# Spans of several edge groups, a wait for the products ahead of the one-hot rows, and a later place for one unit of the graph network

## The reference

```python
# layer 0
edge_input = concatenate([x[dst], x[src], edge_attr, u[batch[dst]]], axis=1)
messages   = relu(edge_input @ W1.T + b1)                      # 200000 x 128
aggregated = segment_sum(messages, dst, num_segments=6250)
out = relu(concatenate([x, aggregated, u[batch]], axis=1) @ W2.T + b2)
x = layernorm(x + out)
# layer 1
h = relu(concatenate([x[src], x[dst], edge_attr], axis=-1) @ msg_w1 + msg_b1)
messages = h @ msg_w2 + msg_b2
mean = segment_sum(messages, dst) / maximum(counts, 1)         # counts: edges of a node
out = relu(concatenate([x, mean], axis=-1) @ upd_w1 + upd_b1) @ upd_w2 + upd_b2
x = layernorm(x + out)
```

## Time and profile before

| what | us |
|---|---|
| median of 3 runs | 4737.94 (4737.09 to 4750.91) |
| profiled execution | 4797.05 |
| its span in the trace | 4795.3 |
| PE matmul busy | 3389.9 (71%) |
| PE weight loads busy | 3156.9 (66%) |
| POOL busy | 2958.2 (62%) |
| DVE busy | 1628.8 (34%) |
| ACT busy | 593.8 (12%) |

### The profile page before, as it was taken

How to read it: one execution, slowest core, us unless ns; L and a number is a source line. 1 busy time by engine, 2 the same in 40 slices (tenths; PEclk the granted TensorE clock), 3 DMA queues, 4 the chain that set the end, 5 groups by cost and what they waited for, 6 DMA issues and landing times.

```text
span 4795.3 us, 47299 instructions
## 1 busy us (share of the span) xinstructions
PE 3389.9 (71%) x16937; PEld 3156.9 (66%) x16937; DVE 1628.8 (34%) x4012; ACT 593.8 (12%) x1017; POOL 2958.2 (62%) x3156
## 2 busy tenths in 40 slices
PE   5777777777777677777746766677677777666767
PEld 4676666666676667767646666666666666666666
DVE  4333333333333333333423333333333223223223
ACT  1110111111111111111111111111111111111111
POOL 5666666656666666666556666666666666666663
PEclk7555555555555555555665555555555555555555
DMA  6443333433334334334423333334334334433432
GB/s 206 123 141 115 114 115 104 118 113 119 114 119 120 117 107 123 120 114 120 127 90 116 115 116 116 117 118 127 115 112 120 117 117 119 118 118 113 122 118 87
DMA packets 291344, 567.98 MB, mean 118 GB/s; under 512 B 166870, under 2 KB 186817, under 8 KB 266140
## 3 DMA queue, kind: packets, MB, share of 16 engines
q1 hardware_dynamic: 168120, 339.88, 21.7%
q0 software_dynamic: 100032, 205.00, 16.4%
q10 hardware_dynamic: 22948, 20.00, 1.3%
HBM read 545.15 MB, written 19.45 MB: 118 GB/s over the span
## 4 chain that ended last, share of the span: by engine, by line
PE 62%; issue 25%; another core or an unknown queue 9%; DVE 2%; DMA 1%; SPq 0%; ACT 0%; DVEq 0%; ACTq 0%
PE bank L1052 26%; PE bank L1066 24%; PE bank L1057 7%; DMA BIG<-in_dstR 1%; DVE BIG L1316 1%; PE bank L997 1%; PE bank L959 1%; PE bank L991 1%; PE bank L972 0%; PE bank L1002 0%; PE bank L1015 0%; PE bank L1037 0%; PE bank L1028 0%; DMA BIG<-tabP 0%
## 5 line engine op out<-in xcount | busy, mean ns | idle before, releaser
L283 POOL DMA_INDIRECT Qr<-tabQ,srcE x3106 | 2936.2, 945 | 1785.1 <-issue 879.6
L1066 PE MATMUL bank<-BIG 128*128 128x42 f32 x6252 | 1433.1, 386 | 645.5 <-issue 642.9
L1066 PEld LDWEIGHTS bank<-BIG 128*128 128x128 f32 x6252 | 1395.8, 312 | 687.9 <-issue 685.0
L1052 PE MATMUL bank<-wall,BIG 128*128 128x128 f32 x6252 | 1590.3, 420 | 319.0 <-issue 306.7
L1052 PEld LDWEIGHTS bank<-wall,BIG 128*128 128x128 f32 x6252 | 1380.7, 315 | 361.7 <-issue 360.8
L1316 DVE TENSOR_TENSOR BIG<-bank,Qr 128x512 f32<-128x512 f32 (+1 forms) x782 | 536.1, 686 | 1572.0 <-remote 1295.0
L1211 ACT ACTIVATE BIG<-BIG 128x512 f32<-128x512 f32 (+1 forms) x782 | 492.2, 629 | 3820.5 <-DVE BIG L1316 3136.1
L1057 PE MATMUL bank<-BIG 126*128 126x128 bf16 x3126 | 515.4, 299 | 307.6 <-issue 290.9
L1057 PEld LDWEIGHTS bank<-BIG 126*128 126x128 bf16 x3126 | 377.9, 140 | 390.8 <-issue 323.6
L1334 DVE TENSOR_TENSOR AC<-AC,bank 128x84 f32 (+1 forms) x782 | 167.8, 215 | 1326.2 <-remote 946.6
L1226 DVE TENSOR_TENSOR BIG<-bank,BIG 126x512 bf16<-126x512 f32 x782 | 533.9, 683 | 149.6 <-DMA BIG<-in_dstR 81.0
(11 more groups left out here) (132 smaller groups left out, 605.7 us busy)
## 6 DMA issues: line engine op xcount, KB each, us to landing
BIG<-in_eaT SPq DMA_DIRECT2D x194, 1024.0 KB
BIG<-in_dstR SPq DMA_DIRECT2D x194, 504.0 KB
Qr<-tabQ,srcE POOLq DMA_INDIRECT x3106
BIG<-tabP SPq DMA_DIRECT2D x782, 31.5 KB
tabP<-BIG ACTq DMA_DIRECT2D x22, 384.0 KB
tabQ<-BIG ACTq DMA_DIRECT2D x17, 256.0 KB
X<-in_xN SPq DMA_DIRECT2D x1, 3136.0 KB
out<-BIG ACTq DMA_DIRECT2D x11, 256.0 KB
```

The lines of the kernel that those rows point to most:

```text
L283: e.indirect_dma_start(Q[0:p, i % R_Q, j, :], None, tabQ[l][:, :], bass.IndirectOffsetOnAxis(ap=srcE[0:p, g, j:j + 1], axis=0)).then_inc(f ...
L1052: e.matmul(bank[i % R_C][:, j * D:(j + 1) * D], f_eaT[:, k % R_EA, (g % LQ * J + j) * P:(g % LQ * J + j + 1) * P], wc[l], start=(j == 0), ...
L1066: last = e.matmul(bank[4 + i % 2][:, 0:W], M[:, i % R_M, j, :], S[:, i % R_S, j, :], start=(j == 0), stop=(j == n - 1))
```

## The change

**Windows.** The groups of a layer are put into 263 windows that share one span of 42 nodes: 26 windows of four groups (g under 104), 50 of two (104 to 203), 187 of one. The rows of `tabP` are loaded once a window (782 loads become 526), PE accumulates A over a window in one bank and counts its edges once, in layer 0 (391 count matmuls become 263), DVE adds a window once (782 acc become 526) and sums S once a window, over up to sixteen one-hot columns in place of four. The ring of S grows from six groups to eight. Waits for acc (v_ag) stand only where a window has been completed.

**The wait.** DVE waited for C of group g-1 right before M of g-1. It now waits for it ahead of ST of g+1, in the same iteration.

**Unit 12.** LAST_BUT_ONE puts its steps later: on ACT behind the relu of the last group, on DVE in layer 1 behind the last acc and the mean of unit 13.

```diff
-R_EA, R_PB, R_BC, R_Q, R_ST, R_S, R_M, R_PT, R_U = 2, 4, 2, 10, 3, 6, 3, 4, 2
+R_EA, R_PB, R_BC, R_Q, R_ST, R_S, R_M, R_PT, R_U = 2, 4, 2, 10, 3, 8, 3, 4, 2
...
+FOURS, PAIRS = 26, 50
+WIN = [(4 * k, 4) for k in range(FOURS)] + [(4 * FOURS + 2 * k, 2) for k in range(PAIRS)]
+WIN += [(g, 1) for g in range(4 * FOURS + 2 * PAIRS, NG)]
...
-LAST_BUT_ONE = [{"y0": 1, "x1t": 4, "q1": 5, "root": 1, "norm": 2, "xt": 5, "copies": 7, "mid": 9, "p_store": 11,
-                 "first": 1, "second": 2, "rest": 7, "lo": 10},
-                {"hidden": 2, "y1": 2, "relu": 1, "root": 2, "norm": 3, "mean": 1, "first": 2, "second": 3}]
+LAST_BUT_ONE = [{"y0": 1, "x1t": 4, "q1": 5, "root": 2, "norm": 3, "xt": 5, "copies": 7, "mid": 9, "p_store": 11,
+                 "first": 2, "second": 3, "rest": 7, "lo": 10},
+                {"hidden": 2, "y1": 3, "relu": 2, "root": 7, "norm": 8, "mean": 1, "first": 5, "second": 7}]
...
-                    if i >= R_PB:
-                        e.wait_ge(v_C, i - R_PB + 1)
-                    e.dma_start(PB[0:K, i % R_PB, :], tabP[l][bass.ds(at[g % LQ], W), :].rearrange("w (h d) -> (w h) d", d=D)).then_inc(f_pb[i % R_PB], 16)
+                    if first_of(i):
+                        w = window(i)
+                        if w >= R_PB:
+                            e.wait_ge(v_C, window_end(w - R_PB))
+                        e.dma_start(PB[0:K, w % R_PB, :], tabP[l][bass.ds(at[g % LQ if len(at) > 1 else 0], W), :].rearrange("w (h d) -> (w h) d", d=D)).then_inc(f_pb[w % R_PB], 16)
...
-                        if l == 0:
-                            last = e.matmul(bank[4 + i % 2][:, W:2 * W], onesb[:, :], S16[:, i % R_S, :], start=True, stop=True)
+                            last = e.matmul(sums[:, 0:W], M[:, i % R_M, j, :], S[:, hot(i), j, :],
+                                            start=(j == 0 and first_of(i)), stop=(j == n - 1 and last_of(i)))
+                        if l == 0 and last_of(i):
+                            last = e.matmul(sums[:, W:2 * W], onesb[:, :], S16[:, w % R_S, :], start=True, stop=True)
...
+                        if g:
+                            e.wait_ge(v_C, i)
                         if i + 1 < 2 * NG:
                             rows_hot(e, i + 1)
...
-                        e.wait_ge(v_C, i + 1)
+                        if g == NG:
+                            e.wait_ge(v_C, i + 1)
                         e.wait_ge(f_q[i % R_Q], q_count(i))
...
-                    if 3 <= g < NG + 3:
+                    if 3 <= g < NG + 3 and last_of(l * NG + g - 3):
```

More of the change, by code:

```diff
@@ L50, with first_of, last_of, window @@
 NU = len(UN)
+FOURS, PAIRS = 26, 50
+WIN = [(4 * k, 4) for k in range(FOURS)] + [(4 * FOURS + 2 * k, 2) for k in range(PAIRS)]
+WIN += [(g, 1) for g in range(4 * FOURS + 2 * PAIRS, NG)]
+NWIN = len(WIN)
+WIN_OF = [w for w, (_, n) in enumerate(WIN) for _ in range(n)]
+def first_of(i):
+    l, g = divmod(i, NG)
+    return g == WIN[WIN_OF[g]][0]
+def last_of(i):
+    l, g = divmod(i, NG)
+    return g == sum(WIN[WIN_OF[g]]) - 1
+def window(i):
+    l, g = divmod(i, NG)
+    return l * NWIN + WIN_OF[g]
+def window_end(w):
+    return w // NWIN * NG + sum(WIN[w % NWIN])
+def windows_done(i):
+    return window(i) if i < 2 * NG else 2 * NWIN
 def edges_below(node):
@@ L55, in edges_below @@
     return E * p + 6 * math.sqrt(E * p * (1 - p))
[L58 removed]
+READY = [window_end(WIN_OF[math.ceil(edges_below((b + n) * P) / GE) - 1]) for b, n in UN[:-1]] + [NG]
 BASE = [g + 3 for g in READY[:-2]] + [READY[-2] + 1, NG + 2]
@@ L1054, in fast_tensor @@
                         for j in range(tiles(g)):
-                            if j == tiles(g) - 1 and i >= 4:
-                                e.wait_ge(v_ag, i - 3)
-                            last = e.matmul(bank[i % R_C][:, j * D:(j + 1) * D], ST[0:K, i % R_ST, j * P:(j + 1) * P], PB[0:K, i % R_PB, :], start=False, stop=(j == tiles(g) - 1))
+                            if j == tiles(g) - 1 and i >= 4 and windows_done(i - 3) > windows_done(i - 4):
+                                e.wait_ge(v_ag, windows_done(i - 3))
+                            last = e.matmul(bank[i % R_C][:, j * D:(j + 1) * D], ST[0:K, i % R_ST, j * P:(j + 1) * P], PB[0:K, w % R_PB, :], start=False, stop=(j == tiles(g) - 1))
                         last.then_inc(v_C, 1)
@@ L1061, in fast_tensor @@
                         if g >= NG and i >= 2:
-                            e.wait_ge(v_ag, i - 1)
+                            e.wait_ge(v_ag, windows_done(i - 1))
                         e.wait_ge(v_rl, i + 1)
                         n = tiles(g - 2)
+                        w = window(i)
+                        sums = bank[4 + w % 2]
                         for j in range(n):
-                            last = e.matmul(bank[4 + i % 2][:, 0:W], M[:, i % R_M, j, :], S[:, i % R_S, j, :], start=(j == 0), stop=(j == n - 1))
-                        if l == 0:
-                            last = e.matmul(bank[4 + i % 2][:, W:2 * W], onesb[:, :], S16[:, i % R_S, :], start=True, stop=True)
+                            last = e.matmul(sums[:, 0:W], M[:, i % R_M, j, :], S[:, hot(i), j, :],
+                                            start=(j == 0 and first_of(i)), stop=(j == n - 1 and last_of(i)))
+                        if l == 0 and last_of(i):
+                            last = e.matmul(sums[:, W:2 * W], onesb[:, :], S16[:, w % R_S, :], start=True, stop=True)
                         last.then_inc(v_A, 1)
@@ L1299, in fast_vector @@
                             rows_hot(e, 0)
+                        if g:
+                            e.wait_ge(v_C, i)
                         if i + 1 < 2 * NG:
                             rows_hot(e, i + 1)
-                        if g > 3:
-                            e.wait_ge(v_ag, i - 3)
+                        if g > 3 and windows_done(i - 3) > windows_done(i - 4):
+                            e.wait_ge(v_ag, windows_done(i - 3))
                         rel = relE[:, g, :].unsqueeze(2).broadcast_to([P, J, W])
                         io = bank[6][:, NGP:NGP + W].unsqueeze(1).broadcast_to([P, J, W])
-                        e.tensor_tensor(S[:, i % R_S, :, :], io, rel, ALU.is_equal).then_inc(v_s, 1)
+                        e.tensor_tensor(S[:, hot(i), :, :], io, rel, ALU.is_equal).then_inc(v_s, 1)
                     if 1 <= g < NG + 1:
                         i = l * NG + g - 1
-                        if l == 0:
+                        if l == 0 and last_of(i):
+                            w = window(i)
+                            h = hot(i) + 1 - WIN[w][1]
                             e.wait_ge(v_s, i + 1)
-                            with nc.allow_low_precision(reason="a sum of four zeros or ones"):
-                                e.tensor_reduce(S16[:, i % R_S, :], S[:, i % R_S, :, :].rearrange("p j w -> p w j"), AX, ALU.add).then_inc(v_cn, 1)
-                        e.wait_ge(v_C, i + 1)
+                            with nc.allow_low_precision(reason="a sum of at most sixteen zeros or ones"):
+                                e.tensor_reduce(S16[:, w % R_S, :], S[:, h:hot(i) + 1, :, :].rearrange("p r j w -> p w (r j)"), AX, ALU.add).then_inc(v_cn, 1)
+                        if g == NG:
+                            e.wait_ge(v_C, i + 1)
                         e.wait_ge(f_q[i % R_Q], q_count(i))
@@ L1323, in fast_vector @@
                         last_terms(e, g // 16)
-                    if 3 <= g < NG + 3:
+                    if 3 <= g < NG + 3 and last_of(l * NG + g - 3):
                         i = l * NG + g - 3
-                        if (g - 3) % LQ == 0:
-                            at = bases(mybir.EngineType.DVE, g - 3)
+                        w = window(i)
+                        if loaded != i // NG * NQ + (g - 3) // LQ:
+                            loaded = i // NG * NQ + (g - 3) // LQ
+                            at = bases(mybir.EngineType.DVE, (g - 3) // LQ * LQ)
                         e.wait_ge(v_A, i + 1)
-                        if i and (g <= 3 or g >= NG):
-                            e.wait_ge(v_ag, i)
-                        if i == NG:
+                        if w and (w == NWIN or g >= NG):
+                            e.wait_ge(v_ag, w)
+                        if w == NWIN:
                             e.wait_ge(s_mz, NU)
-                        acc = AC[:, 0:ctl, bass.ds(at[(g - 3) % LQ], W)]
-                        e.tensor_tensor(acc, acc, bank[4 + i % 2][:, 0:ctl * W].rearrange("p (t w) -> p t w", w=W),
+                        acc = AC[:, 0:ctl, bass.ds(at[(g - 3) % LQ if len(at) > 1 else 0], W)]
+                        e.tensor_tensor(acc, acc, bank[4 + w % 2][:, 0:ctl * W].rearrange("p (t w) -> p t w", w=W),
                                         ALU.add).then_inc(v_ag, 1)
@@ L1491, in laid_out @@
         "dstR": dstp.astype(_np.int16).reshape(1, EP),
-        "base": dstp.astype(_np.int32)[::GE].reshape(1, NGP),
```

(1 more changed line is left out.)

13 lines of the change are left out of this document (9 added, 4 removed).

## The result

The changed kernel takes 4862.71 us (median of 4 runs, 4848.61 to 4871.27), the kernel before 4743.27 us beside it (4 runs): a ratio of 1.0234, 95% interval 1.0211 to 1.0257, thus 119 us slower. The profiled execution of after has a span of 4869.1 us, 74 us more than that of before. The two differ because the profiled execution of before was 54 us above the median of the timed runs of that kernel, that of after only 9.

A forecast was written before the change was run, and what follows sets the result against it. PE and POOL hold each other: PE creeps under gathers, POOL waits 849 us for M. Terms +80 +51 +18 +8 -7 -19 -2 = +129 us on 4738 give 4867 us; range 4700 to 4940, likeliest case 4820 to 4900.

The forecast's parts named there:

- the signs that the prediction set itself: Trace after: POOL's M waits about 980 us, restart 1.8 us after release, bursts 16 and 12; wrong if bursts of 20.
- the term of fewer pauses: Longer pauses let PE do more work, giving POOL longer bursts and fewer pauses: -19 us, bounds 0 and -38.
- The step from 0.96 to 1.80 us: Short pauses: time from PE's release to POOL's restart grows by 0.84 us, ST and S now standing behind the release.
- +80, +51, +18, +8 and -7: In us: ST and S in layer 1, layer 0; layer 0's sum over S, base and wide; pauses beginning with acc.
- My counter-argument: Against fewer pauses: after acc pauses, 1.35 us longer, bursts were 16 and 12 as elsewhere; so half was taken.
- What the spans take away: Saved acc, sums, count matmuls and loads, put at 0 beside the pauses; up to 30 us of PE without cover.
- The -2 us: Unit 12's later place at the layers' ends: last relu right behind M, last acc earlier; from nothing to -3.
- Bursts of 20: Rival: fewer PE steps per group let POOL issue 20 gathers per pause; -85 us, 4653 us; clear case chance 0.12.
- The later M: Rival: PE's release comes earlier by what DVE adds, so only savings count; 4708 to 4736 us, say 4715; chance 0.12.
- Bursts of 12: Rival: one ST less ready, PE creeps less far ahead, POOL issues 12 gathers per pause; +239, 4977 us; chance 0.08.

The follow-up runs named there:

- the gate: Kernel before plus PE waiting in every fourth group for POOL's last issuable gathers: 4624.84 us; with moved wait 4810.14, spans and unit 12 4621.45, whole change 4830.97.
- the pair on one chip: Kernel before with the moved wait alone, and changed kernel with the wait back at M, on a creeping chip: 4885.43 us (1.0272) and 4739.32 us (0.997).

## Why the prediction was right, and where its terms were off

**Direction and size.** 4867 us was forecast, 4862.71 measured; +129 against +119. The cause is the one that was named, and four runs carry it: on the chip that creeps the moved wait alone is slower by 2.7% (+131 us) and the spans without it are not (-15 us), with the gate the wait costs 185 us and the spans -3. Of the signs that the prediction set itself, two failed: POOL's waits for M came to 876 us and not to about 980, and bursts of 20 came, which stood among the signs of being wrong. Both go with the term of fewer pauses below.

**The step from 0.96 to 1.80 us** is right to the row: 0.61 for ST and 0.24 for S in the pause above, 1.80 in 75 of layer 1's 88.

**Longer pauses.** The terms +80, +51, +18, +8 and -7 make +150 for pauses of unchanged number (8 x 0.43 + 4 x 1.29 is 8.6, thus 9 and not 8). In the two profiled executions the mean pause grew from 4.10 to 4.80 us; over 206 pauses that is +144. The sum over S was overestimated (0.35 us on the path and not 0.43; 0.73 and 1.35 for the wide ones, not 0.86 and 1.72).

**Fewer pauses.** By the two profiled executions this is the mis-sized term. I took -19 us, bounds 0 and -38. There are 20 pauses fewer, at 4.8 us -96 us. Bursts of 20 gathers, 3 in the trace of before, became 72. The reason that I had weighed and halved, that the end of PE's full pace goes with POOL's restart, is borne out by the pair on one chip: taken as the start of the last matmul ahead of PE's first idle time of over 0.3 us (in rows 5 and 6 that is 13.3 us after the restart, where the prediction has 13.4), that end lies 14.4 us after the restart in both (medians), but 16.5 us after the release with the moved wait and 15.5 without. It doesn't make the whole of the -96. From before to after the same time rose from 13.2 to 14.7 us, and the spans alone have their 14.4 with a run of 0.96 us; what raised it isn't shown. My counter-argument was misread. In the trace of before 30 of 38 pauses that begin with an acc in layer 0 are followed by 16 gathers, but only 35 of the 65 short ones there; the bursts behind them were longer, 15.2 gathers against 13.3 in the mean. The gated kernels show the other side: where the gate sets the pauses, the wait costs nearly what the rows give, 185 of 201 us.

**Why the sum fitted all the same.** By the profiled pair, waits for M, pauses under issue and the wait between the layers give +69 of the 74 us; the timed runs give 119. The 45 us between them lie in the profiled execution of before, 54 us above its median. How its pauses would divide in an execution at the median isn't known, so how much of the -96 is that can't be settled from this pair: if the 54 us were 13 whole pauses of 4.1 us, 7 fewer would be left, an estimate of -34 us. The pair on one chip has -54 there, with the spans in it. The timed runs on that chip bear out the size: +131 for the wait and -15 for the rest make +116. Part of the agreement to 4 us is chance.

**A wait that I hadn't counted.** Between the layers POOL waits 49.4 us, not 39.8; with the moved wait alone it's 50.2, without it 39.0. In both slower traces POOL's last burst ended with PE still creeping: in after its last gather of the layer ended at 2413.34 and the next M started only at 2417.67, whereas in before PE had been let go at 2385, with three gathers left. Whether this is the wait's doing or where the last burst happened to fall stays open; the gated kernels have 39.6 and 39.5 without the spans, 36.2 and 36.3 with them.

**What the spans take away, put at 0** with up to 30 us if the cover were gone: 15 us less on the chip that creeps (0.997, with unit 12's part in it), none where PE doesn't creep, 3 under the gate. So part of the saved work seems to count where PE creeps, by fewer pauses (193 over 1.5 us, against 206 in the trace of before from another comparison); by which of the saved pieces, no run here shows. The rule of the Trainium skill, "Perfetto Trace Analysis", section "Identifying the Most-Contended Engine", to optimise the engine of highest occupancy first, is not without ground for the spans on the creeping chip: PE is the busiest engine there too. But the trace doesn't agree with it as a guide to this change, as the 131 us of the wait hung on what stands between two engines, with PE busy 70% of the span with it and 71% in the version without it.

**Unit 12.** The relu came where it was expected. The -2 us show on the chip without creep, where the span ends 14.5 and not 16.2 us after the last M. In the profiled execution of after itself nothing was gained: it ended 18.0 us after the last M, that of before 16.4 us. The acc of the last group came 7.5 us after M, with PE busy 10.00 of 10 us at the lower clock (window 4848 to 4858, granted 0.50), where before the clock had gone up (0.76 in the window 4770 to 4780).

**The rivals.** Bursts of 20 came, but beside the longer pauses and not in place of them; without the move 39 came as well, and that kernel was 0.3% faster, far from the 85 us of a clear case. The later M was not absorbed. Bursts of 12 became fewer (44 to 16, by gaps over 1 us). What the prediction didn't ask is whether PE creeps on every chip.

## What to carry to other kernels

Work that an engine can do while it waits belongs ahead of the wait: an instruction moved behind it cost up to its length here each time that wait was the one that held the others, and nothing where it wasn't. To price such a move, count the pauses and read what stands between the release and the restart, but ask also how the cycle answers: with the longer pauses their number fell by a tenth in the profiled pair. And keep two changes apart that come in one diff; here one was worth -0.3% and the other +2.7%, both measured on the same chip.

## What the hardware showed that was not expected

The kernel before takes about 3950 us on two chips (3952.59 and 3945.84) and about 4750 in the first comparison and in the last one (4743.27 and 4754.1), each time with timed runs that agree within 1%. The difference is PE's creep beside POOL's indirect gathers. Counted as three or more idle times of PE of over 0.3 us in close succession, there are some 200 such stretches with a mean of 8.7 us in the trace of before, and three to seven in the traces of the kernels without a gate on the faster chips. Windows in layer 1, the changed kernel on a chip without creep:

```profile
2600.00:2620.00 20.00, 14.83 (x73) 13.63 (x72) 9.06 (x15) 2.21 (x4) 15.12 (x16) 0.50 0.49 148
2620.00:2640.00 20.00, 18.54 (x91) 17.84 (x92) 7.64 (x18) 2.92 (x6) 15.10 (x16) 0.50 0.42 134
```

And on one that creeps, the version without the moved wait:

```profile
2600.00:2620.00 20.00, 10.76 (x51) 9.41 (x50) 5.71 (x7) 0.63 (x1) 12.65 (x14) 0.50 0.43 127
2620.00:2640.00 20.00, 17.41 (x86) 17.28 (x87) 6.13 (x13) 2.52 (x4) 14.43 (x16) 0.50 0.40 126
```

POOL issues 16 gathers in each 20 us on the first, where its waits for M come to 5 us in the whole span; on the second 14 and 16. The granted clock is 0.50 in all four, so it isn't the clock. Where the creep comes from, and whether it stays with a chip or comes and goes there, no run here shows. Measured on one chip alone, the comparison would have shown this change as slower by 2.3% or as no change.
